# Sampling indices of each unit by one broadcast transfer of 1152 KB instead of four of 288 KB

## The chip, the core and the metric

The kernel runs on one core of a Trainium2 chip. The metric is the device time of one execution in microseconds (us), lower is better. The engines are TensorE (PE, with its weight loads shown apart as PEld), VectorE (DVE), ScalarE (ACT), GpSimd (POOL) and SyncE (SP, which here only issues DMAs; its row in a profile is SPq). Sixteen DMA engines move the data.

## What is computed

A small hybrid network on x of shape (4, 16, 16, 32): a deformable-attention convolution, a dynamic convolution, a causal attention, a mixture of experts, a linear attention and a spectral mixer, each added to its input. The change lies in the first block. Its core is a bilinear sampling at computed places:

```python
def deform_sample(img, offset, mask, dilation, pad):
    ...
    y0, x0 = jnp.floor(py), jnp.floor(px)
    def gather(iy, ix):
        valid = ...
        idx = (jnp.clip(iy, 0, h - 1) * w + jnp.clip(ix, 0, w - 1)).astype(jnp.int32)
        g = jax.vmap(lambda f, i: jnp.take(f, i, axis=1))(flat, idx.reshape(b, -1))
        return g.reshape(b, cg, K2, h, w) * valid[:, None]
    out = gather(y0, x0) * (1 - wy_) * (1 - wx_) + ...   # four corners
    return out * mask[:, None]
```

Keys and values are sampled so at 9 places for each of 4 groups, with dilations 1, 3, 5 and 7; then each position attends over its 9 samples.

## The kernel before

The first block works in 8 units (T = 8): unit u is half of one image, 128 positions, one on each partition. For each unit there are J = 36 sampling indices per position (4 groups by 9 places). The gather is done on TensorE by matrices that hold a single one in each column ("one-hots"): DVE compares the unit's indices, copied to all 128 partitions, with the partition's own number (`one_hots`, L1039, in two halves of 18 indices, for both halves of the image), ACT makes the last quarter of one of the two by a distance and a rectifier (`distances`, L747, and `own_one_hots`, L753), and PE multiplies them with a table of keys and values of all four corners (the loop from L1654, 216 matmuls a unit, in 5 groups of at most 8 indices; GRP = 5). After each group PE adds 1 to `s_gp` (in the profile "samples_in_psum"), and ACT copies the group's samples from PSUM to SBUF (`sample_group`, L696). DVE then forms key products (L438), sums (L1067), weights (L1055), value products (L447, three quarters of them by POOL) and value sums (L1091). The order on every engine is written out by hand: while PE gathers unit u, DVE works on units u-1 to u-3 and makes the one-hots of u+1.

The indices come to all partitions in two ways. For unit 0, PE and ACT do it (`index_group`, L681). All indices are also turned into rows and stored to a DRAM tensor `index_rows` (L491), and for the units 1 to 7 SP reads a unit's 36 rows of 128 bf16 back with a stride of zero over the partitions, so that each partition gets the same 9216 bytes. This is the loop that the change touches:

```python
            for u in range(1, T):
                for part in range(PARTS):
                    if u >= 2:
                        sp.wait_ge(s_gp, GRP * (u - 2) + part + 1)
                    js = slice(part * J // PARTS, (part + 1) * J // PARTS)
                    sp.dma_start(ixb[u % 3][:, js, :]..., rows_d[...]...).then_inc(d_ix[u % 3], 16)
```

`ixb` is three buffers, two in the tile `indexb` and one in the tail of `stu_fq`. The first part of unit u waits until the first group of unit u-2 is in PSUM, part 2 until the second group, and so on: four transfers, spaced by one group of PE's work each. The readers (`one_hots` at L1033 and `distances` at L744) wait for all parts of the unit: `index_parts(u)`, which is PARTS times the number of units that have used that buffer's semaphore. SP's next work behind the loop is L508, which waits for ACT's `moe_parts`.

PE also has filler matmuls on the tile `spare` (`occupied`), 9 of them ahead of unit 3, and in some units a few matmuls on weights (`weights_prepared`).

Of the kernel before, what the change touches and what calls it, by code (L numbers as in the profile page):

```python
# [96 lines left out]
def hybrid(nc, x_ch, cst_d, front_d, pw_d, l1_d, attk_d, l2_d, moe_d, moeb_d, l3w_d, l3b_d, l3_d, turn_d, sigma_d, stu_d, toep_d, parity_d, out, DBG=()):  # L97
    with ExitStack() as ctx:
# [307 lines left out]

        groups = lambda u: GRP * (u + 1)
        OWN = J // 4
        PARTS = 4
        index_parts = lambda u: PARTS * ((u + 2) // 3)  # L410

        SB = (2, 3, 4, 5)
# [57 lines left out]
        def _(sp):  # L470
# [22 lines left out]
# [5 lines that stand above are left out]
                    sp.dma_start(ixb[u % 3][:, js, :].rearrange("p j n -> p (j n)"),  # L498
                                 rows_d[u * J:(u + 1) * J, :][js].rearrange("j n -> (j n)").unsqueeze(0).broadcast_to([P, J // PARTS * P]))\
                        .then_inc(d_ix[u % 3], 16)  # L500
# [1622 lines left out]
```

## Time and profile before

| | us |
|---|---|
| median of 3 runs | 226.54 |
| lowest to highest | 225.76 to 226.71 |
| the profiled execution | 226.85 |
| its span in the trace | 225.1 |
| PE busy | 198.4 (88%) |
| DVE busy | 166.2 (74%) |
| ACT busy | 104.4 (46%) |
| data moved by DMA | 17.23 MB |

The span is what the trace covers; the profiled execution's own time is 1.75 us longer. The units of the first block run from about 30 to 90 us of the span. An instruction's row in the timeline gives its start, its duration, its engine, line, operation and tiles, and in brackets how long the engine stood idle before it and what released it; "issue" there is time in which the engine waited for nothing that the profile shows. The profile also lists packets of two queues named "instruction" (q8 and q14) beside the data queue q1.

### The profile page before, as it was taken

What the parts mean: (1) busy time and instruction counts of PE and PEld (TensorE: products, weight loads), DVE (VectorE), ACT (ScalarE), POOL (GpSimd) and SP (SyncE); (2) the same over time, 40 slices, a digit from 0 to 9 for tenths busy, and PEclk for the clock granted to TensorE, in tenths of its full rate; (3) what the DMA queues carried; (4) which work ended last, traced back from release to release, by engine and by line L of the source; (5) the groups of instructions that cost most, each with busy time, mean ns of one, the idle gap of its engine ahead of it and who ended that gap; (6) DMA issues with size and microseconds to landing.
All of it is one profiled execution on the core that took longest, in us unless ns stands there. A gap on an engine that the chain in (4) does not pass through costs nothing.

```text
span 225.1 us, 6720 instructions
## 1 busy us (share of the span) xinstructions
PE 198.4 (88%) x2889; PEld 137.1 (61%) x2889; DVE 166.2 (74%) x371; ACT 104.4 (46%) x264; POOL 37.8 (17%) x53
## 2 busy tenths in 40 slices
PE   7889889999999889997887889869987979989994
PEld 2467478989999888432453375422324556636993
DVE  2599999998999998985882827689699748667001
ACT  2624996859978795331024430320797500046000
POOL 4914000041244034000002004051100000110000
PEclk9999999999999999999999975999999999999999
DMA  6650256534655400102160000300210280000000
GB/s 175 215 171 3 81 180 178 172 114 152 203 147 169 120 6 12 18 2 44 40 185 2 0 3 19 94 15 20 67 36 0 54 341 0 0 0 3 0 0 23
DMA packets 11101, 17.23 MB, mean 77 GB/s; under 512 B 3846, under 2 KB 5789, under 8 KB 10944
## 3 DMA queue, kind: packets, MB, share of 16 engines
q1 hardware_dynamic: 10928, 16.52, 24.9%
q8 instruction: 22, 0.36, 0.7%
q10 hardware_dynamic: 144, 0.30, 0.4%
q14 instruction: 7, 0.06, 0.1%
HBM read 16.03 MB, written 0.78 MB: 75 GB/s over the span
## 4 chain that ended last, share of the span: by engine, by line
PE 41%; DVE 38%; issue 7%; ACT 7%; POOL 4%; DMA 1%; POOLq 0%; DVEq 0%
PE ps L1497 34%; DVE onehot L1039 5%; POOL arena L583 2%; DVE arena L1405 2%; PE ps L1785 2%; DVE arena L1402 2%; PE ps L1786 2%; DVE arena L447 2%; ACT indexb L681 2%; DVE dots L1067 2%; POOL rstd L576 2%; DMA cst<-in_cst 1%; ACT indexb L636 1%; DVE att L1091 1%; DVE arena L438 1%
## 5 line engine op out<-in xcount | busy, mean ns | idle before, releaser
L1497 PE MATMUL ps<-table,onehot 128*128 128x64 bf16 x1728 | 52.7, 193 | 3.6 <-DVE onehot L1039 1.3
L1497 PEld LDWEIGHTS ps<-table,onehot 128*128 128x128 bf16 x1728 | 51.5, 98 | 5.0 <-issue 3.0
L1497 PE MATMUL ps<-spare 128*128 128x512 bf16 (+1 forms) x182 | 49.0, 397 | 5.8 <-ACT onehot L636 1.9
L1497 PEld LDWEIGHTS ps<-spare 128*128 128x128 bf16 x182 | 16.4, 104 | 28.4 <-issue 4.7
L696 ACT ACTIVATE arena<-ps 128x512 f32<-128x512 f32 (+1 forms) x40 | 21.4, 552 | 12.7 <-PE ps L1497 12.4
L1497 PE MATMUL ps<-arena 128*32 128x66 f32 (+5 forms) x380 | 22.7, 255 | 2.0 <-DVE arena L1405 1.5
L447 POOL TENSOR_TENSOR arena<-arena,w4p 128x288 f32<-128x288 f32 x18 | 13.9, 803 | 55.0 <-DVE arena L447 55.0
L1497 PEld LDWEIGHTS ps<-arena 128*32 128x32 f32 (+2 forms) x380 | 19.6, 136 | 4.9 <-DVE arena L1405 2.0
L576 POOL TENSOR_TENSOR rstd<-var_eps,cst 128x4 f32<-128x4 f32 (+2 forms) x9 | 8.8, 982 | 76.7 <-DVE var_eps L916 44.5
L1039 DVE TENSOR_SCALAR onehot<-indexb,cst 128x2304 bf16<-128x2304 bf16 (+1 forms) x24 | 17.8, 772 | 0.4 <-ACT indexb L681 0.4
L636 ACT ACTIVATE indexb<-comp 128x128 bf16<-128x128 f32 x6 | 1.9, 309 | 31.3 <-DVE comp L928 31.3
L438 DVE TENSOR_TENSOR arena<-arena,q_tok 128x1152 f32<-128x1152 f32 x8 | 10.8, 1354 | 1.8 <-ACT arena L696 1.8
L1489 DVE SCALAR_TENSOR_TENSOR table<-ps,window,arena 128x128 f32<-128x128 f32 x2 | 0.6, 347 | 14.1 <-PE ps L1497 14.1
L1067 DVE TENSOR_REDUCE dots<-arena 128x144 f32<-128x1152 f32 x8 | 10.8, 1347 | 0.1
L705 ACT ACTIVATE pexp<-logit,peak 128x9 f32<-128x9 f32 x32 | 9.2, 298 | 3.1 <-DVE peak L1085 3.1
L1091 DVE TENSOR_REDUCE att<-arena 128x32 f32<-128x1152 f32 x7 | 9.4, 1343 | 0.0
L636 ACT ACTIVATE arena<-ps 128x512 f32<-128x512 f32 (+3 forms) x14 | 6.6, 505 | 5.1 <-PE ps L1786 2.4
L753 ACT ACTIVATE onehot<-onehot,pos 128x1152 bf16<-128x1152 bf16 x7 | 8.8, 1252 | 0.0
L1785 PE MATMUL ps<-onehot,indexb 128*128 128x512 bf16 x16 | 6.1, 383 | 1.4 <-DVE arena L1405 0.8
L1785 PE MATMUL ps<-table,indexb 128*128 128x512 bf16 (+1 forms) x24 | 6.8, 322 | 0.5 <-ACT indexb L636 0.3
L1786 PE MATMUL ps<-table,indexb 96*128 96x512 bf16 (+1 forms) x24 | 7.1, 322 | 0.0
L636 ACT ACTIVATE indexb<-ps 128x256 f32<-128x256 f32 (+2 forms) x9 | 4.2, 497 | 4.5 <-PE ps L1778 1.7
(285 smaller groups left out, 346.4 us busy)
## 6 DMA issues: line engine op xcount, KB each, us to landing
indexb<-index_rows SPq DMA_DIRECT2D x20, 288.0 KB, 3.5
stu_fq<-index_rows SPq DMA_DIRECT2D x8, 288.0 KB, 3.5
arena<-in_toep SPq DMA_DIRECT2D x1, 2120.5 KB, 8.1
l<-in_l SPq DMA_DIRECT2D x1, 646.5 KB
onehot<-lin_split SPq DMA_DIRECT2D x6, 96.0 KB
stu_fq<-in_stu SPq DMA_DIRECT2D x1, 560.0 KB, 3.6
table<-stu_split SPq DMA_DIRECT2D x7, 70.0 KB, 1.9
l<-in_l SPq DMA_DIRECT2D x1, 384.0 KB, 6.4
```

Of the source, the lines that this page charges most:

```text
L438: return engine.tensor_tensor(out=prod_k.rearrange("p (g n d) -> p g n d", g=G, d=HC), in0=samples(u, 0).rearrange("p (g s) (n d) -> p g ( ...
L447: ins = engine.tensor_tensor(out=prod_v[u % 2].rearrange("p (g d s n) -> p g d s n", g=G, d=HC, s=K2)[:, g], in0=samples(u, 1).rearrange(" ...
L576: nc.gpsimd.tensor_tensor(out=out_ap, in0=in_ap, in1=exponent, op=ALU.pow).then_inc(g0.sem, g0.step(name))
L636: nc.scalar.activation(out_ap, in_ap, ACT.Copy, scale=scale).then_inc(steps.sem, steps.step(name))
L696: nc.scalar.activation(gv[:, b % 2, :, at:at + count, :], ps[:, SB[n % len(SB)], 0:count * SLOT].rearrange("p (s a d) -> p a s d", s=count ...
L705: ins = nc.scalar.activation(pexp[:, g * K2:(g + 1) * K2], logit[:, g * K2:(g + 1) * K2], ACT.Exp, scale=-1.0, bias=peak[:, g:g + 1], accu ...
L1039: ins = nv.tensor_scalar(ohv[:, u % 2, q, js, :], ixb[u % 3][:, js, :], c["pidx"][:, q:q + 1], None, ALU.is_equal)
L1067: nv.reduce_sum(dots[:], prod_k.rearrange("p (n d) -> p n d", d=HC), axis=AX.X)\
L1091: nv.reduce_sum(tokhb(att[:])[:, h, b, :], prod_v[u % 2].rearrange("p (n k) -> p n k", k=4 * K2), axis=AX.X)\
L1497: return nc.tensor.matmul(out_ap, lhsT, rhs, start=start, stop=stop)
L1785: nc.tensor.matmul(out_ap, l0, r0, start=True, stop=False)
L1786: return nc.tensor.matmul(out_ap, l1_, r1, start=False, stop=True)
```

## The change

One constant: the number of parts in which a unit's indices are fetched goes from 4 to 1.

```diff
@@ -406,7 +406,7 @@
 
         groups = lambda u: GRP * (u + 1)
         OWN = J // 4
-        PARTS = 4
+        PARTS = 1
         index_parts = lambda u: PARTS * ((u + 2) // 3)
```

By it, SP issues 7 transfers in place of 28, each with rows of 9216 bytes in place of 2304. A unit's only transfer waits for what its first part waited for; the waits of the parts 2 to 4 are gone. The readers wait for one arrival in place of four, all of the unit's data in both cases. Buffers, bytes and the work of the other engines stay.

On SP's queue, between the store of the index rows and the store of the experts' weights, the difference is this (`index_rows_stored` is the end of L491's store, `samples_in_psum` is `s_gp`):

```order
 L488 DMA stu_fq<-in_stu 128x1120
 L491 DMA index_rows<-idx_rows 96x3x128 [waits scalar_front]
-L498 DMA indexb<-index_rows 128x1152 [waits index_rows_stored]
-L498 DMA indexb<-index_rows 128x1152 x3
-L498 DMA stu_fq<-index_rows 128x1152 [waits samples_in_psum] x4
-L498 DMA indexb<-index_rows 128x1152 [waits samples_in_psum] x8
+L498 DMA indexb<-index_rows 128x4608 [waits index_rows_stored]
+L498 DMA stu_fq<-index_rows 128x4608 [waits samples_in_psum]
+L498 DMA indexb<-index_rows 128x4608 [waits samples_in_psum] x2
```

The rows of the units 5 to 7 change in the same way. On the engines that read the indices, and on PE, which is waited for, nothing moves:

```order
## PE: 500 rows in the other, 500 in this; the same
## DVE: 323 rows in the other, 323 in this; the same
## ACT: 161 rows in the other, 161 in this; the same
```

## Rows read from the trace of the kernel before

**Rows 1.** The profile's DMA queues: packets, MB, share of 16 engines.

```profile
q8 instruction: 22, 0.36, 0.7%
```

**Rows 2.** The chain that ended last: start us, us, what.

```profile
37.80 6.60 PE ps L1497 x217
44.41 0.30 issue
...
48.76 0.23 issue
48.99 8.96 PE ps L1497 x276
```

**Rows 3.** Timeline of DVE: start us, us, engine, line, tiles, idle before.

```profile
53.45 1.36 DVE L438 TENSOR_TENSOR arena<-arena,q_tok 128x1152 f32<-128x1152 f32 x1 [1.06 <-ACT arena L696]
...
61.10 1.35 DVE L438 TENSOR_TENSOR arena<-arena,q_tok 128x1152 f32<-128x1152 f32 x1
...
68.74 1.35 DVE L438 TENSOR_TENSOR arena<-arena,q_tok 128x1152 f32<-128x1152 f32 x1
```

**Rows 4.** Timeline of SP's queue, the index transfers and what follows them.

```profile
25.39 1.77 SPq L498 DMA_DIRECT2D indexb<-index_rows  x4
31.79 4.52 SPq L498 DMA_DIRECT2D stu_fq<-index_rows  x4
...
84.42 0.33 SPq L508 DMA_DIRECT2D moe_split<-moe_parts  x1
```

**Rows 5.** DMA issues: KB each, median us from issue to landing.

```profile
indexb<-index_rows SPq DMA_DIRECT2D x20, 288.0 KB, 3.5
...
arena<-in_toep SPq DMA_DIRECT2D x1, 2120.5 KB, 8.1
```

**Rows 6.** Line L498 alone in the stretch 26.7 to 28 us: unit 1's last part.

```profile
L498 SPq DMA_DIRECT2D indexb<-index_rows x1: 432/432/432, 26.7 to 26.7; - x1
...
DMA to landing us min/median/max: 4.4/4.4/4.4
```

**Rows 7.** Timeline of ACT, the first readers of unit 1's and unit 2's indices.

```profile
33.69 1.25 ACT L747 ACTIVATE onehot<-indexb,npidx 128x1152 bf16<-128x1152 bf16 x1
...
41.29 1.25 ACT L747 ACTIVATE onehot<-stu_fq,npidx 128x1152 bf16<-128x1152 bf16 x1
```

**Rows 8.** Stretches: us, busy time of each engine, PEclk, DMA share, GB/s.

```profile
40.20:46.80 6.60, 6.20 (x208) 5.84 (x205) 6.30 (x11) 5.25 (x14) 0.00 (x0) 1.00 0.62 185
...
179.00:185.40 6.40, 5.12 (x81) 3.23 (x83) 2.69 (x8) 0.02 (x1) 0.00 (x0) 1.00 0.89 339
```

**Rows 9.** Timeline of PE's weight loads in the units 1 to 5.

```profile
37.77 6.37 PEld L1497 LDWEIGHTS ps<-table,onehot 128*128 128x128 bf16 x216 [0.47 <-ACT arena L696]
...
44.71 0.24 PEld L1497 LDWEIGHTS ps<-l 32*32 32x32 f32 x15 [0.41 <-issue]
...
48.98 3.64 PEld L1497 LDWEIGHTS ps<-table,onehot 128*128 128x128 bf16 x123 [0.35 <-issue]
...
61.76 3.80 PEld L1497 LDWEIGHTS ps<-table,onehot 128*128 128x128 bf16 x128 [0.53 <-issue]
65.77 1.67 PEld L1497 LDWEIGHTS ps<-table,onehot 128*128 128x128 bf16 x55 [0.20 <-issue]
...
74.48 0.52 PEld L1497 LDWEIGHTS ps<-table,onehot 128*128 128x128 bf16 x16 [0.76 <-issue]
```

**Rows 10.** Queues in stretches of 0.2 us from 42.2, 46.6, 50.0 and 62.6 us.

```profile
q8 instruction: 1, 0.02, 31.0%
...
q8 instruction: 1, 0.02, 28.9%
...
q8 instruction: 1, 0.02, 29.9%
...
q8 instruction: 1, 0.02, 41.8%
```

**Rows 11.** Timeline of ACT, the last samples of unit 3.

```profile
59.83 0.87 ACT L696 ACTIVATE arena<-ps 128x512 f32<-128x512 f32 x2
```

## The prediction

> **What bounds the kernel now.** I read the chain that ended last first. In the first block it runs on PE until 57.96 us, apart from the end of DVE's one-hots, and it holds two stretches called "issue", 0.30 us at 44.41 and 0.23 us at 48.76 [rows 2]. After that the chain is DVE's. DVE's own timeline says how firmly: the key products (L438) of the units 2, 3 and 4 start at 53.45, 61.10 and 68.74, the last two steps both about 7.64 us, which is DVE's own work for a unit, with no idle time before them; only the one at 53.45 stood idle, 1.06 us, for ACT's copy of samples, which waits for PE [rows 3]. So PE sets the pace until 53.45, and DVE from there to the end of the units. A microsecond that PE gains ahead of 53.45 is worth a microsecond up to the 1.06 that DVE idles, and a microsecond that it loses there is lost. Behind 53.45 PE has a little slack: unit 3's last samples are copied at 59.83 + 0.87 = 60.70 [rows 11], and DVE takes them at 61.10, 0.40 us later.
>
> The second view is SP's queue and the landings, because that is what the change edits. Nothing in the trace stands waiting for an index transfer: the one idle time in front of the readers is ACT's or PE's, not a DMA's.
>
> The third view is what else the DMA engines carry. Queue q8 moved 22 packets with 0.36 MB, 16 KB each [rows 1]. PE's weight loads show whose they are. Between the stalls at 44.71 and 48.98 lie 128 weight loads, from 61.76 to 65.77 again 128, from 65.77 to 74.48 the 55 of the row shown and 200 of the one behind it, 255 or about twice 128, and each of these stalls is "issue" [rows 9]. A matmul and its weight load are two instructions, so PE crosses a boundary in its code every 256 instructions, and the stall is the wait for the next 16 KB. The same count puts the crossings that did not stall at about 40.4 (127 weight loads of 29.5 ns ahead of the end of unit 1), 53.0 and 57.2. Behind each crossing follows one q8 packet, and the next crossing needs it. The packets started in the 0.2 us from 42.2, 46.6 and 50.0 [rows 10], that is about 1.9, 2.0 and 1.1 us behind the crossings at 40.4, 44.71 and 48.98; and where the stretch was free of index data, at 62.7, only 0.9 us behind 61.76. From a packet's start to the end of the stall it feeds are 44.71 - 42.3 = 2.4 us and 48.98 - 46.7 = 2.3 us. One round is thus 0.9 + 2.4 = 3.3 us on free DMA engines, under the 128 x 30 ns = 3.8 us that PE takes for the code, and 1.9 + 2.4 = 4.3 us beside index data: a stall of about 0.4, as seen. The Trainium skill, "Runtime: NRT & Kernel Launch", section "Instruction fetch mechanics", says that code comes in 16 KiB blocks of 256 instructions and that a crossing is "mostly hidden"; the count agrees with the trace, the hiding does not hold here, at 0.41 and 0.35 us.
>
> **The change, part by part.** First, the issues. SP's 28 issues become 7. Each takes about 0.3 us on SP, and SP has nothing else to do until L508 at 84.42, which waits for ACT [rows 4]. Worth 0, hidden by that wait.
>
> Second, the landing. Unit 1's four parts, all queued at once, are issued from 25.39, and the last one, issued at 26.7, lands 4.4 us later at 31.1: 5.7 us for the same 1152 KB [rows 4, 6]. One large transfer of another tensor, 2120.5 KB, took 8.1 us and ran at 339 GB/s [rows 5, 8]; less its data time of 6.4 us the fixed part is 1.7, and 1.18 MB at that rate are 3.5, together 5.2 us. So I take 5.2 to 5.7 us from issue to landing. The first reader of unit 1 starts at 33.69 [rows 7], 8.3 us behind the issue. Unit 2 is issued at 31.79 and first read at 41.29, 9.5 us later. Now its fourth part, issued at about 36.0, lands 3.5 us later at 39.5 [rows 4, 5]; one transfer lands at about 37.3. Nobody waited for it before, so this is worth 0 too, and the cover is 2.6 us at least, in unit 1. The later units wait for the same kind of signal and stand in the same way.
>
> Third, what the transfers do to PE's code. Now a unit's index data is spread over some 6.6 us of each 7.6 at 62% of the DMA engines [rows 8]; then it comes in one burst of about 3.6 us, starting about 0.85 us behind the issue. The bursts of the units 2 and 3 lie at about 32.6 to 36.3 and 40.2 to 43.9, and that of unit 4, issued when unit 2's first group is done at about 47.5, at 48.3 to 52.0. I go through the crossings ahead of 53.45. The one at 36.4 falls behind its burst: no stall now, none then. The one at 40.4 falls into the start of unit 3's burst: its packet, at 42.3 now, has to get in between packets of 9216 bytes. Now it waits about 1.0 us more than on free engines, although a packet of 2304 bytes takes only about 0.1 us; so what it waits for is not one packet but some 20 KB already taken up by its engine. I expect the same bytes to be ahead of it, plus the rest of one longer packet, 0.4 - 0.1 = 0.3 us. The stall of 0.41 becomes 0.7: +0.3. The crossing at 44.71 then has free engines, the burst being over: its packet comes after 0.9, and the stall of 0.35 at 48.98, 0.23 of it on the chain, goes: -0.3. The crossing at 48.9 falls into unit 4's burst: 2.2 + 2.4 = 4.6 us against the 3.9 to the next crossing at 53.0, a new stall of 0.7, which stands in the fillers and the start of unit 3, where 0.4 of slack takes most of it: +0.3. Behind that the stalls at 61.76 and 74.48 may grow by some tenths, on the side of PE that has 0.4 us and more, and that at 65.77 goes: 0.
>
> The sum is 0 + 0 + 0.3 - 0.3 + 0.3 = +0.3 us, against the profiled execution's 226.85: 227.15. That execution lies 0.31 above the median of the runs, so I predict **226.9**. Bounds of the unknown part, the code's wait, are -0.76, both stalls gone (0.41 + 0.35, below the 1.06 that DVE idles), and the end of the burst, below.
>
> **The rivals.** The first: the code's packet gets its turn at once, between two index packets. Then each crossing in a burst waits 0.9 + 0.4 = 1.3 us at most, the round is 3.7, under 3.8, and both stalls go: 226.54 - 0.76 = 225.8, gain limited by DVE, which is the bound from 53.45 on. Against it stands that the crossings at 40.4 and 44.71 waited 1.9 and 2.0 us among packets of 0.1 us. This is what the Trainium skill's "DMA: Bandwidth & Descriptors", section "Queues, rings and completion order", would have: the engine round-robins between queues at the granularity of a packet. The trace does not bear it out for packets as short as these.
>
> The second, slower: the code's packet waits until its DMA engine has emptied the whole transfer. In favour: the packets at 46.6 and 50.0 stand in lulls of the index data, and 46.6 is where the data of unit 3 ends. Then the packet for the crossing at 40.4 starts at 43.9, the code is there at 46.3 against 44.3, a stall of 2.0 in place of 0.41: +1.6. The stall at 48.98 goes, -0.3. Unit 4's burst, moved back with PE, holds the next packet to its end, and the code comes 1.9 late, less 0.4 of slack: +1.5. From there each unit costs PE 6.4 us for its matmuls and such a stall of about 1.8, 8.2 and with the weights' matmuls up to 8.7, against DVE's 7.64: up to 0.5 to 1.0 for unit 4 and 5 each, less slack, together about +0.8. The sum is +3.6, less if a crossing misses its burst: 229 to 230, say 229.8. It decides when the wait passes about 1.5 us beyond the free one, since then a stall of some 1 us appears at each of two crossings.
>
> The third: the one transfer is slow and the readers wait. It would have to take over 8.3 us from issue to landing. At the rate of a part on its own, 4 x 3.5 = 14 us, unit 1 would be 5.7 us late, and each unit on; 240 and more. Unit 1's own four parts in 5.7 us speak against it.
>
> That the change does nothing at all to the order is nearly so: only SP's queue differs, and what is left is the traffic's shape.
>
> **How the numbers follow.** The forecast has 0.50, the first rival 0.15, the second 0.28 with everything between it and the forecast, the third 0.02, and 0.05 is left for effects without a name, 0.03 of it faster. A measurement of this kernel can tell about 0.5%, 1.13 us, from no change: 225.41 to 227.67. The forecast and the first rival both lie inside it; the forecast's upper end (0.3 us more at three crossings) reaches the edge, so I count 0.04 of it as slower. Faster by more than that needs more than the two stalls: those 0.03 and 0.02 of the first rival, 0.05. Slower: 0.28 + 0.02 + 0.04 + 0.02 = 0.36. Same: 0.59. The range goes from the first rival, 225.8 less 0.1, to nearly the second, 229.4.
>
> **What would show it.** In the trace of the changed kernel: seven issues on SP with a landing of 5 to 6 us; no idle time of DVE or ACT with a DMA as its end; the "issue" stall at about 49 gone; one of 0.5 to 1 us at about 44.5 and a new one near 53; DVE's idle time before its key product of unit 2 still about 1 us. If the stalls at 44 and 53 are 1.5 us or more, the second rival holds, and the q8 packets then stand at the ends of the bursts; if both stalls are gone and DVE idles 0.3, the first. The prediction is wrong if a reader waits for the transfer, or if PE's matmuls or DVE's instructions change in length beside the denser traffic, for which the trace of before gives no sign.

## The result

The changed kernel takes **233.32 us** (median of 4 runs, 231.34 to 236.23) against 226.62 us for the kernel before in the same comparison. One of the four runs, the one of 236.23, was in a slower state of the chip, and the ratio leaves it out: 1.027, with a 95% interval of 1.021 to 1.034. So the change makes the kernel slower by 2.7%, some 6.2 us, and the time lies outside the range of 225.7 to 229.4. The profiled execution took 234.02 us with a span of 232.1, 7.0 more than the 225.1 of before.

The index transfers are issued as predicted. From the DMA issues of the changed kernel's page (KB each, median us from issue to landing), then SP's queue:

```profile
indexb<-index_rows SPq DMA_DIRECT2D x5, 1152.0 KB, 5.7
stu_fq<-index_rows SPq DMA_DIRECT2D x2, 1152.0 KB, 6.3
```

```profile
25.41 0.34 SPq L498 DMA_DIRECT2D indexb<-index_rows  x1
31.80 0.34 SPq L498 DMA_DIRECT2D stu_fq<-index_rows  x1
39.39 11.58 SPq L498 DMA_DIRECT2D indexb<-index_rows  x2
59.68 0.32 SPq L498 DMA_DIRECT2D stu_fq<-index_rows  x1
68.22 6.62 SPq L498 DMA_DIRECT2D indexb<-index_rows  x2
```

There are seven issues; the row "39.39 11.58 x2" is two issues with SP's wait between them. Over all seven, issue to landing takes 5.6 to 7.3 us. ACT, the first reader of unit 2's indices, starts at 41.29 as before [rows 7], and no idle time of DVE or ACT in the units ends on a DMA.

The chain that ended last shows where the time went (start us, us, what). It answers to [rows 2]:

```profile
37.80 6.60 PE ps L1497 x217
44.40 1.95 issue
46.35 0.40 PE ps L1497 x13
...
46.79 9.27 PE ps L1497 x239
56.07 1.57 issue
57.64 8.21 PE ps L1497 x255
65.84 1.72 issue
67.56 7.63 PE ps L1497 x256
...
75.30 3.91 PE ps L1497 x128
79.21 2.84 issue
```

Before, "issue" stood twice on the chain, with 0.30 and 0.23 us, and then the chain was DVE's. Now it stays on PE, and "issue" takes 1.95, 1.57, 1.72 and 2.84. Between these pieces lie 255, 256 and 128 matmuls: they are the same crossings of PE's code as before. PE's weight loads, which answer to [rows 9], show the stall as the idle time in brackets:

```profile
46.35 0.24 PEld L1497 LDWEIGHTS ps<-l 32*32 32x32 f32 x15 [2.06 <-issue]
...
47.73 7.67 PEld L1497 LDWEIGHTS ps<-table,onehot 128*128 128x128 bf16 x216
...
57.63 0.33 PEld L1497 LDWEIGHTS ps<-spare 128*128 128x128 bf16 x4 [1.85 <-issue]
...
67.57 7.50 PEld L1497 LDWEIGHTS ps<-table,onehot 128*128 128x128 bf16 x255 [1.82 <-issue]
...
82.04 0.52 PEld L1497 LDWEIGHTS ps<-table,onehot 128*128 128x128 bf16 x16 [2.96 <-issue]
```

Where the code's packet stands decides between the prediction and its second rival. The data of unit 3 keeps the queues busy from 40.2 us on. These are the DMA queues (packets, MB, share of the 16 engines) in the slices of 0.2 us from 43.8 and from 44.0:

```profile
q1 hardware_dynamic: 8, 0.07, 86.8%
...
q1 hardware_dynamic: 10, 0.03, 34.5%
q8 instruction: 1, 0.02, 31.4%
```

In none of the slices between 40.2 and 44.0 is there a q8 packet. The one that the crossing at 40.4 asked for comes in the slice in which the data runs low. It does not wait for the very last row: the stretch from 45.05 to 46.3 us, about 1 us later, still holds three packets, two rows of 9216 bytes and the transfer's last one of a few bytes:

```profile
q1 hardware_dynamic: 3, 0.02, 5.7%
```

The q8 packet takes 31.4% of 16 engines' time in 0.2 us, which is 1.0 us of one engine. That fits an engine which moved the code ahead of its last two rows of data. So the code holds the data up too: the transfers of the units 3 and 4, behind whose code packets such rows come, land 7.3 us after their issue, the others 5.6 to 6.4. Nobody waits for them. It is the same in the later bursts: data until 55.6, 64.8, 73.2 and 79.4 us, and q8 packets in the slices from 55.4, 65.2, 72.8 and 79.4.

What it costs can be read at DVE's key products (L438), which answer to [rows 3]; the units 2 to 5, then 7:

```profile
56.22 1.36 DVE L438 TENSOR_TENSOR arena<-arena,q_tok 128x1152 f32<-128x1152 f32 x1 [3.85 <-ACT arena L696]
...
65.25 1.36 DVE L438 TENSOR_TENSOR arena<-arena,q_tok 128x1152 f32<-128x1152 f32 x1 [1.30 <-ACT arena L696]
...
73.79 1.36 DVE L438 TENSOR_TENSOR arena<-arena,q_tok 128x1152 f32<-128x1152 f32 x1 [0.82 <-ACT arena L696]
...
83.14 1.36 DVE L438 TENSOR_TENSOR arena<-arena,q_tok 128x1152 f32<-128x1152 f32 x1 [1.62 <-ACT arena L696]
...
96.68 1.36 DVE L438 TENSOR_TENSOR arena<-arena,q_tok 128x1152 f32<-128x1152 f32 x1 [0.52 <-ACT arena L696]
```

Together they idle 3.85 + 1.30 + 0.82 + 1.62 = 7.59 us, where before it was 1.06: 6.5 more. Before, the last of them was this row of DVE's timeline:

```profile
89.91 1.36 DVE L438 TENSOR_TENSOR arena<-arena,q_tok 128x1152 f32<-128x1152 f32 x1 [0.53 <-ACT arena L696]
```

It starts at 96.68 now, 6.77 later, and the span is 7.0 longer. So nearly all of the loss of the profiled execution is made in the units. For the experiments I use one length, from the start of PE's first gather matmul (30.20 before, 30.21 after) to the start of DVE's key product of unit 7: **59.7 us before, 66.5 after**. I call it the length of the units. It is steadier than a single run's time, since the clock in later stages differs a little between executions.

One part of the loss I had not foreseen at all. Unit 2's 216 weight loads take 7.67 us, while unit 1's take about 6.4 [rows 9]. The stretches around them (us, busy time and instructions of PE, PEld, DVE, ACT, POOL, then the granted clock in parts of full speed, DMA share, GB/s):

```profile
47.40:48.40 1.00, 1.00 (x13) 0.81 (x12) 0.97 (x2) 0.00 (x0) 1.00 (x2) 0.50 0.08 16
48.40:50.40 2.00, 2.00 (x43) 2.00 (x40) 2.00 (x4) 0.00 (x0) 1.16 (x2) 0.50 0.00 0
50.40:51.40 1.00, 1.00 (x39) 1.00 (x37) 1.00 (x3) 0.60 (x1) 0.00 (x0) 1.00 0.00 0
```

Some 0.6 us behind the stall of 2.06 us the granted clock falls to 0.50, the lower of its two levels (1.2 GHz), until about 50.4 us. Two microseconds then hold 43 matmuls; the one at full clock behind them holds 39.

### The profile page after: what moved, and what is told of

Same layout as the page of the kernel before. It is cut to its first block, busy times and chain, and to the rows that moved or that the text cites. A ratio compares the mean times of both kernels' runs of the same rounds, so it can differ in the third digit from the quotient of the medians.

```text
span 232.1 us, 6699 instructions
## 1 busy us (share of the span) xinstructions
PE 199.7 (86%) x2889; PEld 138.0 (59%) x2889; DVE 166.4 (72%) x371; ACT 104.1 (45%) x264; POOL 37.9 (16%) x53
## 4 chain that ended last, share of the span: by engine, by line
PE 47%; DVE 31%; issue 8%; ACT 7%; POOL 4%; DMA 1%; POOLq 0%; DVEq 0%
PE ps L1497 40%; POOL arena L583 2%; DVE arena L1405 2%; PE ps L1785 2%; DVE arena L1402 2%; PE ps L1786 2%; DVE onehot L1039 2%; ACT indexb L681 2%; POOL rstd L576 2%; DVE arena L447 2%; DMA cst<-in_cst 1%; ACT indexb L636 1%; DVE att L1091 1%; DVE arena L438 1%; DVE comp L1369 1%
## 5 line engine op out<-in xcount | busy, mean ns | idle before, releaser
L1497 PEld LDWEIGHTS ps<-table,onehot 128*128 128x128 bf16 x1728 | 52.4, 99 | 7.2 <-issue 6.6
L447 POOL TENSOR_TENSOR arena<-arena,w4p 128x288 f32<-128x288 f32 x18 | 13.9, 800 | 61.8 <-DVE arena L447 61.8
L576 POOL TENSOR_TENSOR rstd<-var_eps,cst 128x4 f32<-128x4 f32 (+2 forms) x9 | 8.8, 982 | 76.7 <-DVE var_eps L916 44.5
L438 DVE TENSOR_TENSOR arena<-arena,q_tok 128x1152 f32<-128x1152 f32 x8 | 10.8, 1356 | 8.3 <-ACT arena L696 8.3
L705 ACT ACTIVATION_READ_ACCUMULATOR pexp<-logit,peak 128x1 f32 x32 | 6.4, 201 | 0.0
```

The source lines that it names most:

```text
L438: return engine.tensor_tensor(out=prod_k.rearrange("p (g n d) -> p g n d", g=G, d=HC), in0=samples(u, 0).rearrange("p (g s) (n d) -> p g ( ...
L447: ins = engine.tensor_tensor(out=prod_v[u % 2].rearrange("p (g d s n) -> p g d s n", g=G, d=HC, s=K2)[:, g], in0=samples(u, 1).rearrange(" ...
L576: nc.gpsimd.tensor_tensor(out=out_ap, in0=in_ap, in1=exponent, op=ALU.pow).then_inc(g0.sem, g0.step(name))
L705: ins = nc.scalar.activation(pexp[:, g * K2:(g + 1) * K2], logit[:, g * K2:(g + 1) * K2], ACT.Exp, scale=-1.0, bias=peak[:, g:g + 1], accu ...
L1497: return nc.tensor.matmul(out_ap, lhsT, rhs, start=start, stop=stop)
```

## Experiments

All kernels below start from the kernel before, except where the diff says otherwise. Times are medians with the lowest and highest run, and the ratio is to the kernel before on the same chip, with its 95% interval.

The questions, in the order of the runs: does the code's packet wait for what is queued ahead of it, or for the length of the packets; does the place of the burst decide; what is the unit of the waiting; and is the lower clock behind the stall the code's or only the standstill's. Each expectation names its theories.

### Four transfers again, all at once

The bytes and packets of before, but queued together like the one transfer.

```diff
-                        sp.wait_ge(s_gp, GRP * (u - 2) + part + 1)
+                        sp.wait_ge(s_gp, GRP * (u - 2) + 1)
```

> Four transfers of 288 KB as before, but all four wait only for the first group of unit u-2, so that a unit's 1152 KB are queued within about 1.3 us, in packets of 2304 bytes. Theory A, a packet of PE's code waits until its DMA engine has worked off all the index data that is queued, whatever the length of the packets: like the changed kernel, 231 to 235 us, an issue stall of 1.3 to 2.5 us at about 44.4 and others of over 1 us behind it, the code packets at the ends of the bursts. Theory B, the long packets of 9216 bytes are what holds the code up: no burst of long packets, so 225.8 to 227.5 us and stalls of at most 0.8 us.

Measured: 229.94 us (228.07 to 231.81, 4 runs), ratio 1.013 (1.005 to 1.021); the units last 62.1 us. PE's weight loads:

```profile
45.41 0.24 PEld L1497 LDWEIGHTS ps<-l 32*32 32x32 f32 x15 [0.97 <-issue]
...
54.24 0.33 PEld L1497 LDWEIGHTS ps<-spare 128*128 128x128 bf16 x4 [0.93 <-issue]
```

And the queues in the 0.2 us from 42.8, in the middle of the burst:

```profile
q1 hardware_dynamic: 35, 0.08, 97.6%
q8 instruction: 1, 0.02, 29.2%
```

The time lies between the ranges of both theories. Packets of 2304 bytes suffice for new stalls: their length isn't needed. But here the packet does not wait for the end of the burst. Its crossing lies at 40.59 (127 weight loads of 29.5 ns ahead of 44.34). The four parts are issued at 39.54, 39.91, 40.39 and 40.86, and the slices up to 42.8 hold 251 of the 576 q1 packets of the burst: the code comes when about two parts are moved, counted over all 16 engines, although three were issued ahead of the crossing, the third by 0.2 us. In the next burst it is much the same: 310 of 576 packets up to 51.8, and the code in the slice from there.

The third burst is another case. Its four parts are issued from 56.28 to 57.61, all of them 0.6 us or more ahead of the crossing at 58.2 (124 weight loads behind 54.58). These are the queues from 57.2 to 61.8 us, then in the 0.2 us from 61.8, and the stall that this code packet feeds:

```profile
q1 hardware_dynamic: 575, 1.18, 76.3%
```

```profile
q8 instruction: 1, 0.02, 30.8%
```

```profile
64.17 7.50 PEld L1497 LDWEIGHTS ps<-table,onehot 128*128 128x128 bf16 x255 [1.81 <-issue]
```

Here the code comes behind 575 of 576 packets, all four transfers, and the stall of 1.81 us is as long as the changed kernel's at this place (1.82). So the packet waits for the index data that is queued when PE crosses, be it one transfer or four; what is issued close to the crossing can fall on either side of it.

### Long packets, paced

Four transfers of 288 KB as before, spaced as before, but each brings whole rows of 9216 bytes to 32 partitions.

```diff
-                    js = slice(part * J // PARTS, (part + 1) * J // PARTS)
-                    sp.dma_start(ixb[u % 3][:, js, :]..., rows_d[...][js]...broadcast_to([P, J // PARTS * P]))
+                    ps_ = slice(part * P // PARTS, (part + 1) * P // PARTS)
+                    sp.dma_start(ixb[u % 3][ps_]..., rows_d[...]...broadcast_to([P // PARTS, J * P]))
```

> Four paced transfers of 288 KB per unit as before, each waiting for one group more, but cut by partitions: each brings the whole row of 9216 bytes to 32 partitions. Packets as long as in the changed kernel, the traffic spread as before. Theory A: as before, 226 to 228 us, stalls in the units of at most 1 us. Theory B: slow like the changed kernel, 230 us or more, with stalls of 1.5 us and more.

Measured: 226.56 us (225.95 to 227.68, 10 runs), ratio 1.000 (0.997 to 1.003); the units last 59.7 us, as before. The largest stall in front of unit 3:

```profile
48.93 1.16 PEld L1497 LDWEIGHTS ps<-table,onehot 128*128 128x128 bf16 x38 [0.62 <-issue]
```

The packet's length by itself falls as a cause: packets as long as those of the changed kernel cost nothing when their transfers are small and spaced. Nor is it a fixed number of packets that the code lets pass: that was at most 144 in the changed kernel and 575 in the third burst above.

### One transfer, started two groups later

```diff
-        PARTS = 4
+        PARTS = 1
...
-                        sp.wait_ge(s_gp, GRP * (u - 2) + part + 1)
+                        sp.wait_ge(s_gp, GRP * (u - 2) + 3)
```

> One transfer of 1152 KB per unit as in the changed kernel, but issued when the third group of unit u-2 is in PSUM, about 2.8 us later (34.6 for unit 2, 42.1 for unit 3). Theory A: the stalls move with the bursts. Unit 2's burst lies at about 35.4 to 39, over PE's code crossing at 36.4, so a stall of 0.7 to 1.5 us appears inside unit 1 near 40.4, where neither kernel had one; the stall at the end of unit 1 is then not the long one of 2.06, since its packet is asked for about 41 and served before or at the start of unit 3's burst. In all 228 to 235 us. A rival C, that the place in PE's program makes the stall (the tiny matmuls on weights behind unit 1) and not the traffic: the stall of about 2 us stays at 44.4 and there is none at 40.4.

Measured: 233.75 us (232.81 to 234.60, 4 runs), ratio 1.032 (1.026 to 1.039); the units last 67.2 us. The stalls moved:

```profile
42.34 3.76 PEld L1497 LDWEIGHTS ps<-table,onehot 128*128 128x128 bf16 x127 [1.62 <-issue]
...
51.98 3.64 PEld L1497 LDWEIGHTS ps<-table,onehot 128*128 128x128 bf16 x123 [1.89 <-issue]
...
76.28 5.63 PEld L1497 LDWEIGHTS ps<-table,onehot 128*128 128x128 bf16 x144 [2.83 <-issue]
```

Unit 2's transfer is issued at 34.86, 3 us later than in the changed kernel, and its burst now holds up the code for the crossing at 40.7. PE stalls inside unit 1, where the changed kernel has none (1.62 us, a little over the 0.7 to 1.5 expected), and no longer at 44. The stalls follow the bursts, whatever PE and DVE do at that place. A mere shift gains nothing, since a burst of 4 us against crossings 3.8 us apart always catches one.

### The changed kernel again, on this chip

> The changed kernel once more, as the measure for the three others on this chip: 231 to 235 us, stalls of about 2 us at 44.4, near 57, near 67 and near 81. If the clock drop behind the first stall (granted clock 0.50 from 47.4 to 50.4) belongs to the stall, it appears again when PE stands about 2 us there.

Measured: 233.58 us (232.97 to 234.64), ratio 1.032 (1.026 to 1.038); the units last 68.1 us. The weight loads of unit 2 and the stall ahead of them:

```profile
46.98 0.24 PEld L1497 LDWEIGHTS ps<-l 32*32 32x32 f32 x15 [2.60 <-issue]
...
48.04 8.00 PEld L1497 LDWEIGHTS ps<-table,onehot 128*128 128x128 bf16 x216
```

The loss is the same on a second chip, with the lower clock behind the first stall again. It comes a second time here: the stall that ends at 82.94 is 3.23 us long, and the granted clock is 0.50 from 82.4 to 85.8.

### No index transfers behind unit 2

The floor: only the units 1 and 2 get their indices by DMA. The units 3 to 7 sample with what lies in their buffers, so the output is wrong.

```diff
-        index_parts = lambda u: PARTS * ((u + 2) // 3)
+        index_parts = lambda u: PARTS if u % 3 else 0
...
-            for u in range(1, T):
+            for u in range(1, 3):
```

> Leaves out the index transfers of the units 3 to 7; these units use the indices that lie in their buffer (those of the units 0, 1 and 2), so they sample other places and the output differs. Everything else is the kernel before. The floor for all theories on the index traffic: no issue stall over 0.3 us behind 40 us, 0.5 to 1 us faster than before, 225.4 to 226.1 us, DVE's idle time before unit 2's key product 0.2 to 0.4 us.

Measured: 225.79 us (224.71 to 226.61, 10 runs), ratio 0.997 (0.994 to 1.000); the units last 58.8 us. DVE's key product of unit 2, whose bracket was 1.06 before and 3.85 in the changed kernel:

```profile
52.67 1.36 DVE L438 TENSOR_TENSOR arena<-arena,q_tok 128x1152 f32<-128x1152 f32 x1 [0.16 <-ACT arena L696]
```

Without index data there is no code stall in the units 1 to 6. So all the code stalls of the changed kernel, 6.5 us on DVE with the lower clock behind the first, come from these transfers, and so do 0.9 us of the kernel before. It also bounds what any better order of them can gain: 59.7 - 58.8 = 0.9 us.

### Whole units behind a crossing

If the packet waits only for transfers that are already there, one that is issued just behind the request costs nothing until the next request, 3.8 us later. Here each unit comes as two transfers of 576 KB back to back, issued when the group that ends just behind a crossing is done (groups 2, 5, 7, 10 and 21; the two halves of unit 6 apart, at 16 and 18). `PARTS` is 2, `indices` issues the halves, `buffer_free` waits for the last readers of the buffer.

```diff
-            for u in range(1, T):
-                for part in range(PARTS):
-                    if u >= 2:
-                        sp.wait_ge(s_gp, GRP * (u - 2) + part + 1)
+            indices(1, (0, 1))
+            for u, parts, group in ((2, (0, 1), 2), (3, (0, 1), 5), (4, (0, 1), 7), (5, (0, 1), 10),
+                                    (6, (0,), 16), (6, (1,), 18), (7, (0, 1), 21)):
+                if u >= 3:
+                    buffer_free(u)
+                sp.wait_ge(s_gp, group)
+                indices(u, parts)
```

> All 1152 KB of a unit at once (two transfers of 576 KB back to back), but each issued just behind a point where PE crosses into its next 16 KB of code (groups 2, 5, 7, 10 and 21 of all groups for the units 2, 3, 4, 5 and 7; unit 6 in two halves at groups 16 and 18), so that PE's request for code is already queued. Buffers are taken as early as their one-hots allow. Theory D, first come first served: a code packet waits for the index data that was issued before its request and for no more. Then no issue stall of over 0.3 us is left in the units, DVE's idle time before unit 2's key product falls from 1.06 to about 0.3, and the time is 225.2 to 226.3 us. Theory A', any burst of 1152 KB stalls the code: 229 to 234 us, stalls of over 1.5 us.

Measured: 226.45 us (225.03 to 229.74, 12 runs), ratio 0.999 (0.995 to 1.002); the units last 61.3 us. Two stalls are left:

```profile
41.32 3.76 PEld L1508 LDWEIGHTS ps<-table,onehot 128*128 128x128 bf16 x127 [0.80 <-issue]
...
50.70 3.64 PEld L1508 LDWEIGHTS ps<-table,onehot 128*128 128x128 bf16 x123 [1.45 <-issue]
```

Whole units in one dense burst, and the units last 5 to 7 us less than in the three runs with one transfer (66.5, 67.2 and 68.1), because the bursts start behind crossings, come in pieces, or both: the four parts at once, not placed, came to 62.1, so this run alone does not separate the two. A theory by which any dense burst of 1152 KB costs the same falls. My expectation of no stall at all missed too, and the trace says why. A unit's data takes some 4 us, longer than the 3.8 to the next crossing, so that one half of unit 4 was still being moved at the crossing at 45.16. Unit 5's first half was issued at 45.29, just behind it, and the q8 packet came in the slice from 48.4, when 970 packets were moved from 34.2 on, 864 of them those of the units 2 to 4: 106 of unit 5's 288, ahead of its second half. So the order is not strictly by the time of issue: a transfer that starts within some tenths of a microsecond of the crossing can still go first. With the bursts of the four parts at once, what fits is **the data that is queued at the crossing, give or take one transfer issued close to it**.

### Two halves

```diff
-        PARTS = 4
+        PARTS = 2
...
-                        sp.wait_ge(s_gp, GRP * (u - 2) + part + 1)
+                        sp.wait_ge(s_gp, GRP * (u - 2) + 2 * part + 1)
```

> Two transfers of 576 KB per unit, issued at the first and the third group of unit u-2. Theory D: PE's request at the crossing of 40.4 waits for one half, issued at 39.4, until about 42.1, a stall of 0.2 to 0.5 at 44.4; that at 44.4 comes when the second half is nearly done, that at 48.4 waits for one half until about 50: no stall of over 0.6 us in the units 1 to 3, and 225.8 to 227.3 us. If instead the harm grows evenly with the size of a burst (four spaced parts 0, one transfer +7 us): +2 to +3, 228.3 to 229.5 us.

Measured: 227.49 us (225.18 to 228.12, 10 runs), ratio 1.003 (1.000 to 1.007); the units last 60.6 us. The stall ahead of unit 2:

```profile
45.69 0.24 PEld L1497 LDWEIGHTS ps<-l 32*32 32x32 f32 x15 [1.19 <-issue]
```

I had expected none above 0.6 us. The first half's data runs out at about 43.0, and the code's packet comes at 43.2, where quarters let it through at 42.2 [rows 10] and the whole only at 44.0. The stall grows with the size of one transfer: 0.41, 1.19 and 2.06 us for 288, 576 and 1152 KB.

### Halves, each behind a crossing

The version that follows from this, again with `PARTS = 2`: unit 2 right behind unit 1, while PE doesn't yet wait for code, and then one 576 KB half behind each crossing. One half waits for a mark behind its group too, `wd2`, so as to come behind its crossing at 44.3.

```diff
+            indices(1, (0, 1))
+            indices(2, (0, 1))
+            for u, part, group in ((3, 0, 2), (3, 1, 5), (4, 0, 7), (4, 1, 10), (5, 0, 12), (5, 1, 16),
+                                   (6, 0, 18), (6, 1, 21), (7, 0, 24), (7, 1, 27)):
+                buffer_free(u)
+                sp.wait_ge(s_gp, group)
+                if (u, part) == (4, 1):
+                    sp.wait_ge(tw.sem, tw["wd2"])
+                indices(u, (part,))
```

> Two transfers of 576 KB per unit, each alone behind one crossing of PE's code (unit 2 right after unit 1; then one half at each of the groups 2, 5, 7, 10 with the first weight product of unit 2, 12, 16, 18, 21, 24 and 27). Theory D, first come first served by transfers: each half is moved before the next request for code, so no issue stall over 0.3 us is left in the units 1 to 7, and DVE starts unit 7's key product 58.8 to 59.2 us behind PE's first gather, as in the kernel without the late transfers (58.8) and against 59.7 before; 225.4 to 226.3 us, 0.1 to 0.5% under before. If halves do harm of themselves (as in the kernel of two halves, 227.5 us, 60.6): 227 us or more.

Measured: **226.24 us** (224.82 to 227.13, 12 runs) against 226.92 us, ratio 0.997 (0.994 to 0.999); the units last 58.8 us. DVE's key product of unit 2 and unit 2's weight loads:

```profile
52.66 1.36 DVE L438 TENSOR_TENSOR arena<-arena,q_tok 128x1152 f32<-128x1152 f32 x1 [0.16 <-ACT arena L709]
...
45.39 6.45 PEld L1510 LDWEIGHTS ps<-table,onehot 128*128 128x128 bf16 x216
```

The halves are issued at 37.13, 40.96, 44.81 and 48.55, each with nothing queued in front, and the code's packets come in the slices from 37.8, 41.2, 45.4 and 48.8. The halves are as large as those of the kernel with two halves (60.6 us), so the 1.8 us between the two are the place's. All the index data is moved, and the length of the units is that of the kernel which moves none behind unit 2. The whole 0.9 us of the kernel before is recovered in the units, and this kernel beats both, the one before by 0.3%, just clear of the noise.

### A standstill made by hand

Is the lower clock behind a stall something of the code, or of PE standing still? Here PE waits for DVE's weights of an earlier unit ahead of unit 2, with the transfers of before.

```diff
                 elif u == 2:
+                    pe.wait_ge(v1.sem, v1["w4p0"])
                     values_by_dense(2)
```

> The kernel before, with one wait more: PE stands behind unit 1 until DVE's weights of unit 0 (L1055) are done at about 46.5, so that it is idle from 44.2 to 46.5, as long as in the changed kernel, with the index traffic as before. If the clock drop there comes from PE standing still, whatever it waits for: granted clock about 0.5 between 47 and 50, unit 2's 216 weight loads in about 7.7 us in place of 6.4, and 1.9 us of idleness less 0.4 to 0.6 for hidden code stalls plus 1.3 for the clock, together 228.6 to 230 us. If the clock drop needs more than the idle time: weight loads in 6.4 us and 227.5 to 228.3 us.

Measured: 228.75 us (228.46 to 231.77, 4 runs), ratio 1.014 (1.007 to 1.020); the units last 61.3 us. PE stood still longer than in the changed kernel (2.46 us against 2.06), but its clock stayed up. The time would have fitted the other theory (228.6 to 230 us); the weight loads decide:

```profile
46.75 0.24 PEld L1497 LDWEIGHTS ps<-l 32*32 32x32 f32 x16 [2.46 <-DVE w4p L1055]
...
47.84 6.45 PEld L1497 LDWEIGHTS ps<-table,onehot 128*128 128x128 bf16 x216
```

The loss, 1.6 us of length, is nearly what DVE's idle time rose by (2.57 in front of its key product of unit 2, against 1.06). So 2.46 us of standstill do not always lower the clock.

The same with a longer wait (`v1["dots1"]` in place of `v1["w4p0"]`), one run:

> As idle_by_hand, but PE waits for DVE's sums of unit 1 (L1067, done at about 48.3), so it stands still for about 4 us behind unit 1. If a standstill of PE of itself lowers the clock once it is long enough: granted clock about 0.5 in the 2 or 3 us behind it and unit 2's 216 weight loads in 7.5 us or more. If not: 6.4 us, as in idle_by_hand.

Measured: 231.88 us, units 64.6 us long. The weight loads, and a stretch in the middle of them:

```profile
48.49 0.24 PEld L1497 LDWEIGHTS ps<-l 32*32 32x32 f32 x16 [4.21 <-DVE dots L1067]
...
49.58 8.00 PEld L1497 LDWEIGHTS ps<-table,onehot 128*128 128x128 bf16 x216
```

```profile
50.00:52.00 2.00, 2.00 (x42) 2.00 (x40) 2.00 (x5) 0.00 (x0) 0.00 (x0) 0.50 0.00 0
```

A wait for DVE of 4.21 us does what the code stall of 2.60 did: the same 8.00 us for unit 2's loads, at a granted clock of 0.50. The lower clock therefore needs no code stall; here it followed a plain wait. What decides between 2 and 3 us stays open. Code stalls of 2.06, 2.60, 2.83 and 3.23 us were followed by slower loads (7.67, 8.00, 5.63 for 144 in the kernel with the later start, there at a clock of 0.50 from 76.4 to 78.4, and 0.88 for 16 in the repeated kernel). The one of 2.96 was not (a clock of 1.00 from 82 to 84), nor were the one of 2.10 in the kernel with the later start (1.00 from 87.6 to 90.6) and the wait of 2.46.

## Why the prediction was wrong

**The issues were right, and so was what the landing is worth.** 7 issues, no reader that waits, hidden by the cover that was named. The landings themselves were longer than said, 5.6 to 7.3 us against 5.2 to 5.7. The third rival is out.

**The count of the crossings was right**, and it is what made the trace readable: the stalls lie at the places named, about 44.5 and in the fillers ahead of unit 3.

**The step that failed is the code's wait at the crossing at 40.4**: "not one packet but some 20 KB already taken up by its engine. I expect the same bytes to be ahead of it, plus the rest of one longer packet", +0.3. It took the 1.0 us that the packet waited before [rows 10] for a fixed amount of bytes. But what it waited for was the index data queued ahead of it: in the kernel before little more than one part of 288 KB (171 packets from 40.2 to 42.2, where a part has 144), with the change 1152 KB. The stall went from 0.41 to 2.06, +1.65. The two halves and the four parts at once lie between, at 1.19 and 0.97. The rows in hand could not tell the two readings apart, as every transfer of before in that stretch had one size; but they could not support the forecast either, and there the fault of the weights lies: 0.50 for a fixed amount and 0.28 for the whole transfer, with the second supported by the packets at 46.6 and 50.0 that stood in lulls, and the first by nothing of its own.

**The first rival** (the packet gets its turn between two index packets) falls by the empty slices from 40.2 to 44.0. The prediction set beside it the Trainium skill's "DMA: Bandwidth & Descriptors", section "Queues, rings and completion order": each engine takes turns between queues, packet by packet. I read "packet" as the profile counts packets, one row of 2304 or 9216 bytes. The same section gives a packet as typically 9 to 17 descriptors; an engine's share of one index transfer is 128 / 16 = 8 rows in both kernels, so in the page's sense a whole transfer is one packet, and its rule would give about the second rival's wait, not the first's. Read so, the trace nearly agrees for the single transfer (code in the slice from 44.0, two rows behind it). For several transfers in a row it does not: about two parts, and in one burst all four, were moved ahead of the code.

**The second rival had the mechanism, and its first term almost exactly**: packet at 43.9 (seen from 44.0), code at 46.3 (46.35), stall 2.0 (2.06). It gave 229.8, 3.5 us under the median. Its terms against what they measured, on the path to DVE:

| term | second rival | measured |
|---|---|---|
| stall ahead of unit 2 | +1.6 | 2.06 - 0.41 = +1.65 |
| the stall at 48.98, gone | -0.3 | -0.23 |
| clock of 0.50 behind the stall | none | +1.36 |
| unit 3 | +1.5 | +1.30 |
| units 4 and 5 | +0.8 | 0.82 + 1.62 = +2.44 |
| rest, to the last key product | | +0.25 |
| sum | +3.6 | +6.77 |

The clock's term is from the end of the stall to DVE's key product of unit 2: 56.22 - 46.35 = 9.87 us now, 53.45 - 44.71 - 0.23 = 8.51 before. Two terms were thus mis-sized. The clock was left out, although a stall of 2 us was forecast in that rival; the trace of before has no such standstill in the units, and I took its full clock for granted. And the units 4 and 5 were costed with a stall of about 1.8 each less slack, whereas the one in unit 5 is 2.96: there the burst, issued at 74.5, has its data right behind the crossing at 75.30, so that the packet waits for all of it. It was sized from a typical place of the burst, not from the worst. The bursts are also 4.0 us long, at 283 GB/s in the stretch from 51.4 to 55.4, not 3.6.

A stall's size can be worked out from this. The packet starts about where the data queued ahead of it ends, or 0.9 us behind the crossing if none is; the code is there 2.3 us later; PE needs it 3.8 us behind the crossing. With a burst that ends at 44.1 and the crossing at 40.4: 44.1 + 2.3 - 40.4 - 3.8 = 2.2 (2.06 measured). With one that ends at 79.4 and the crossing at 75.30: 79.4 + 2.3 - 75.3 - 3.8 = 2.6 (2.96).

**The chances.** Slower by over 0.5% had 0.36, same 0.59. The range ended where the second rival ended, 229.4, short even of its own 229.8, and it had no case in which both of the rival's open sizes went badly together. With a stall of 2.9 us in place of 1.8 in each of the units 4 and 5, as a burst right behind a crossing makes it, its end would have been 229.8 + 2.2 = 232, still short of the median. (The forecast's own sum, 227.15 less 0.31, is 226.84; it was rounded up to 226.9.)

**What is shown and what is argued.** Shown: the stalls are PE's code (they vanish with the index data, and come at multiples of 128 matmul pairs), they depend on how much index data is queued at a crossing and when, and not on the length of its packets, and they go when each half follows a crossing alone. That the code comes behind what is queued at the crossing is drawn from where the q8 packets stand in five kernels. Why a transfer issued within some tenths of a microsecond of the crossing sometimes goes first and sometimes not stays open; the counts are over all 16 engines, and no view tells which engine moved a packet.

The Trainium skill's "Runtime: NRT & Kernel Launch", section "Instruction fetch mechanics", says of crossings that they are "mostly hidden". The trace agrees in the stretches without index data (no stall behind unit 2 with the transfers left out) and disagrees beside a large transfer, at 1.1 to 3.2 us each. The Trainium skill's "DMA: Bandwidth & Descriptors", section "Bandwidth", advises transfers of 1 MiB and more; by that rule this change should be harmless or a gain, and here it costs 2.7%, because the transfers were hidden anyway and something else stood behind them in line.

## What to carry to other kernels

Before you merge background transfers into a large one, look for what small and urgent traffic shares the DMA engines with them: PE's code above all, where a kernel is unrolled and its matmuls are short. "Issue" stalls at equal distances of 128 matmul pairs, and packets on the "instruction" queue, are its signs. Then the data that is queued when PE crosses into its next 16 KB, and not its packets' length, sets how late the code comes: one large transfer, or several small ones issued together (four at once cost 1.81 us too, where all were queued in time). The remedy is smaller transfers, each issued just behind a crossing with none in front of it. And where a stall of some 2 us is forecast for PE, put the lower clock behind it among the costs; here it added 1.36 us behind the first stall.

## What the runs showed of the hardware

- A packet of PE's code comes behind the index data that is queued when PE crosses: behind 575 of 576 packets where all four parts were issued 0.6 us or more ahead of the crossing, behind 251 and 310 of 576 where the third was issued 0.2 us ahead of it. For a crossing at 40.4 to 40.6 it came at 44.0 us behind one transfer of 1152 KB, at 43.2 behind a half, at 42.8 inside a burst of four quarters, and at 42.2 among paced quarters.
- Packets of 9216 bytes in small, spaced transfers delay it no more than those of 2304 (ratio 1.000, 0.997 to 1.003).
- The code's packet of 16 KB takes about 1.0 us of one DMA engine and can hold up data: two rows came behind it, and those transfers landed 7.3 us after their issue instead of 5.6 to 6.4.
- PE's granted clock fell to 0.50 for about 3 us around or behind standstills of 2.06, 2.60, 2.83 and 3.23 us for code and of 4.21 us for DVE, and stayed at 1.00 behind ones of 2.10, 2.46 and 2.96. For 216 weight loads that is 7.7 to 8.0 us in place of 6.45.
